# Attention and expert layer: transpose of the combine weights moved within slot 3, expert choice in slot 3, all engine programs without loops

## The reference, cut to what matters

```python
x = x + _L0_attn_ref(_layernorm(x), Wqg, Wkv, Wout)
x = x + _L0_ffn_ref(_layernorm(x), gate_kernel, gate_bias, w_gate, w_up, w_down, ...)
# in the second:
topk_idx, topk_weight = _gate(x, gate_kernel, gate_bias)      # 2 of 4 groups, then 4 of 16 experts
combine = jnp.einsum('nke,nk->ne', onehot, topk_weight)
inter = jax.nn.silu(g) * u                                    # all 16 experts are computed
y = jnp.einsum('ne,enh->nh', combine, jnp.einsum('enm,emh->enh', inter, w_down))
```

## Time and profile before

| | before |
|---|---|
| runs, median (lowest to highest) | 830.85 us (829.86 to 833.11) |
| profiled execution, own time | 831.47 us |
| its span, first to last instruction | 829.5 us |
| PE busy / weight loads | 691.8 us (83%) / 545.1 us (66%) |
| DVE busy | 520.7 us (63%) |
| ACT busy | 434.9 us (52%) |
| POOL busy | 352.7 us (43%) |
| granted clock of PE, mean | 0.920 |
| DMA, mean | 73 GB/s |

### The profile page before, as it was taken

One profiled execution on the slowest core, in us unless ns is written; L12 is line 12 of the kernel. 1 busy time (PEld: TensorE's weight loads), 2 busy tenths in 40 slices (PEclk: granted clock), 3 DMA queues, 4 the chain that ended last, 5 costly groups with the idle time before them and its releaser, 6 DMA issues.

```text
span 829.5 us, 16902 instructions
## 1 busy us (share of the span) xinstructions
PE 691.8 (83%) x5160; PEld 545.1 (66%) x5160; DVE 520.7 (63%) x1739; ACT 434.9 (52%) x986; POOL 352.7 (43%) x368
## 2 busy tenths in 40 slices
PE   1576897979979797988979797997979799797785
PEld 1444476858767685867758585876758587676675
DVE  3545667576666748576575757667475856666654
ACT  2466674565646464564646456464655556453211
POOL 2246563644435353544535264453526444363100
PEclk9878998999989898998989899898989999898898
DMA  8994849091835619092562909174371908300000
GB/s 194 132 144 48 131 87 108 14 144 24 124 48 95 72 60 113 6 139 32 94 72 73 98 18 137 24 113 58 79 87 36 128 1 126 40 15 1 8 7 7
DMA packets 72814, 60.94 MB, mean 73 GB/s; under 512 B 8624, under 2 KB 72496, under 8 KB 72752
## 3 DMA queue, kind: packets, MB, share of 16 engines
q1 hardware_dynamic: 72752, 60.26, 49.4%
HBM read 41.37 MB, written 18.87 MB: 73 GB/s over the span
## 4 chain that ended last, share of the span: by engine, by line
PE 57%; DVE 25%; issue 9%; ACT 4%; DMA 2%; DVEq 1%; POOL 1%; SPq 1%; ACTq 0%; POOLq 0%
PE ps_a L503 11%; PE ps_f L365 8%; PE ps_f L428 7%; PE ps_f L367 6%; PE ps_f L366 6%; PE ps_f L447 5%; PE ps_s L474 5%; PE ps_f L424 4%; DVE norms_m L741 2%; PE ps_f L407 2%; DMA qkt<-qk_rows 2%; DVE it L852 2%; PE ps_f L418 2%; DVE norms_t L661 2%; DVE norms_t L662 2%
## 5 line engine op out<-in xcount | busy, mean ns | idle before, releaser
L334 POOL TENSOR_TENSOR p<-r 128x512 f32<-128x512 f32 x256 | 262.5, 1046 | 392.4 <-ACT r L603 392.4
L603 ACT ACTIVATE r<-ps_s 128x512 f32<-128x512 f32 x256 | 138.5, 596 | 81.0 <-PE ps_s L474 79.8
L503 PE MATMUL ps_a<-p,v 128*64 128x256 f32 x1024 | 143.5, 396 | 3.4 <-DVE big L897 2.2
L897 DVE TENSOR_TENSOR big<-ps_a,wt 128x256 f32<-128x256 f32 x128 | 53.7, 420 | 73.7 <-ACT big L612 51.1
L503 PEld LDWEIGHTS ps_a<-p,v 128*64 128x64 f32 x1024 | 64.4, 138 | 41.7 <-POOL p L334 2.7
L852 DVE TENSOR_TENSOR it<-ps_f,it 128x256 f32<-128x256 f32 x144 | 59.1, 420 | 44.0 <-ACT it L595 41.0
L595 ACT ACTIVATE it<-ps_f 128x256 f32<-128x256 f32 x144 | 55.2, 383 | 50.1 <-PE ps_f L367 47.7
L418 PE MATMUL ps_f<-ident,cs 128*32 128x128 f32 x32 | 9.2, 387 | 83.8 <-DVE cs L787 83.8
L447 PE MATMUL ps_f<-wdown,it 128*128 128x128 f32 x576 | 71.2, 279 | 2.9 <-DVE it L869 1.7
L869 DVE TENSOR_TENSOR it<-ps_f,it 128x512 f32<-128x512 f32 x64 | 44.0, 690 | 44.8 <-PE ps_f L424 44.3
L447 PEld LDWEIGHTS ps_f<-wdown,it 128*128 128x128 f32 x576 | 68.4, 195 | 4.5 <-DVE it L869 1.8
(11 more groups left out here) (153 smaller groups left out, 1607.2 us busy)
## 6 DMA issues: line engine op xcount, KB each, us to landing
qk_rows<-qk_parts SPq DMA_DIRECT2D x16, 1024.0 KB, 4.4
qkt<-qk_rows SPq DMA_DIRECT2D x64, 256.0 KB, 9.5
qkt<-qk_rows SPq DMA_DIRECT2D x128, 128.0 KB, 8.9
x_in<-in_L_attn_tokens SPq DMA_DIRECT2D x16, 128.0 KB, 2.2
x_res<-in_L_attn_tokens SPq DMA_DIRECT2D x16, 128.0 KB, 14.4
out<-o_sb SPq DMA_DIRECT2D x16, 128.0 KB, 14.2
big<-in_L_attn_Wqg SPq DMA_DIRECT2D x1, 640.0 KB, 4.2
big<-in_L_attn_Wkv SPq DMA_DIRECT2D x1, 640.0 KB, 5.3
```

The source lines that it names most:

```text
L334: pool.tensor_tensor(p[h % 4][:], r[h % 2][:], r[h % 2][:], ALU.mult).then_inc(probs_done, 1)
L503: last = pe.matmul(ps_a[k % 2][64 * e:64 * e + 64, 0:N], v[q][:, t, h * DV:(h + 1) * DV], p[h % 4][:, t * N:(t + 1) * N], start=(t == 0), ...
L603: act.activation(r[h % 2][:], ps_s[h % 2][:], ACT.Relu).then_inc(relu_done, 1)
L897: dve.tensor_tensor(aw[ap][:, pair, :], ps_a[pair % 2][:, 0:N], wt[ap][:, pair, :], ALU.mult)\
```

## The change

It takes cT from the head of PE's slot 3 to its end, behind rT, and cB 0 from slot 3 into slot 4, between gu 8 and rB 2. As ACT evacuates in the order of `FILL`, its copy of cT moves too. On DVE `route_experts` moves from slot 2 into slot 3, behind `head_scales`, `gate_up` 5, `gated_heads` of pair 2 and `gate_up` 6; `gate_up` 7 then comes ahead of `value_scales`, and `scale_hidden` 0 goes from the head of slot 4 to a place behind `gate_up` 8. PE, ACT, DVE and POOL are written out for all 20 steps. No instruction is added to or taken from the computation, and no DMA moves.

```diff
-        [("F", "cT", 0), ("F", "gu", 6), ("P", "g", 1), ("F", "gu", 7), ("O", "rT", 0), ("F", "cB", 0)],
-        [("O", "rB", 0), ("O", "rB", 1), ("F", "gu", 8), ("O", "rB", 2), ("O", "rB", 3), ("P", "g", 2)],
+        [("F", "gu", 6), ("P", "g", 1), ("F", "gu", 7), ("O", "rT", 0), ("F", "cT", 0)],
+        [("O", "rB", 0), ("O", "rB", 1), ("F", "gu", 8), ("F", "cB", 0), ("O", "rB", 2), ("O", "rB", 3), ("P", "g", 2)],
...
-        def run_steps(eng, step):
-
-            for s in range(FIRST_STEP, LOOP_FROM):
-                step(s, s % 2, stages(s), s)
-            with eng.Fori(LOOP_FROM // 2, LOOP_TO // 2) as i:
-                step(i * 2, 0, ALL, None)
-                step(i * 2 + 1, 1, ALL, None)
-            for s in range(LOOP_TO, LAST_STEP + 1):
+        def run_flat(step):
+
+            for s in range(FIRST_STEP, LAST_STEP + 1):
                 step(s, s % 2, stages(s), s)
...
@@ DVE
                         if F:
-                            gate_up([4])
-                            route_experts(link_f, fb)
-                            link_f.end()
+                            gate_up([4, 5])
                     if k == 3:
                         if O:
                             head_scales(link_o, b)
                             link_o.end()
+                        gated_heads(k)
                         if F:
-                            gate_up([5])
-                        gated_heads(k)
+                            gate_up([6])
+                            route_experts(link_f, fb)
+                            link_f.end()
+                            gate_up([7])
                         if P_on:
                             value_scales(link_p, s + 1, rq2[pq])
                             link_p.end()
-                        if F:
-                            gate_up([6, 7])
                     if k == 4:
-                        if F:
-                            scale_hidden([0])
                         if O:
                             scale_heads([0, 1])
                         gated_heads(k)
                         if F:
                             gate_up([8])
+                            scale_hidden([0])
                         if O:
                             scale_heads([2, 3])
```

More of the change, by code:

```diff
@@ L351, in step @@
                                 .then_inc(v_normed, 1)
-            run_steps(pool, step)
+            run_flat(step)
         @block.tensor
@@ L506, in step @@
                         last.then_inc(values_done, 1)
-            run_steps(pe, step)
+            run_flat(step)
         @block.scalar
@@ L627, in step @@
                         gates(j, s, q)
-            run_steps(act, step)
+            run_flat(step)
         @block.vector
@@ L1011, in step @@
                                .then_inc(read["x2T"], 1)
-            run_steps(dve, step)
+            run_flat(step)
 _INS = ["L0_attn_tokens", "L0_attn_Wqg", "L0_attn_Wkv", "L0_attn_Wout", "L0_ffn_gate_kernel", "L0_ffn_gate_bias",
```

## The result

The changed kernel takes 826.67 us (median of 17, 819.51 to 830.99), the kernel before 831.15 us (median of 17, 829.86 to 833.80). The ratio is 0.9937 with a 95% interval of 0.9921 to 0.9953. So it is faster by 4.5 us where I had forecast 17, and it just clears the 0.5% that I took as the bound: 826.67 is inside the range of 802 to 827, at its very end. One thing of the runs matters for all that follows. The changed kernel's executions lie 11.5 us apart, those of before 4, and the profiled one, at 819.51 us, is the shortest of the 17.

The account below looks back on a forecast made before the run. PE and DVE taking turns at `cs` was taken as the bound, the loop as second cost. Loop 8, order 5 and last steps 3 us made 16 us off 831.5 (profiled), so 814 us by the median, range 802 to 827.

Parts of the forecast that it names:

- What bounds the kernel: PE and DVE take turns, meeting at PE's wait for `cs`, 83.8 us in 16 waits; loop back edges are second.
- The loop: Writing out the looped steps 4 to 14 was to give 8 us, between 5 and 20.
- DVE's piece: DVE's work ahead of `cs` was to grow by 2.4 us a step, or 1.6 without a second POOL hold.
- PE's piece: From cT to the values of pair 4: 9.35 us before, 5.7 after plus 0.42 per us at half clock.
- The new waits: PE was to wait some 45 us for `cs`, about 14 for `rs` at rT, 15 for `gate_up` 3 at gu 6.
- The clock: Half clock (1.2 GHz) behind cT was to average 2 us a full step, costing 11 us over 13 steps.
- the gain of 16: New order's gain before half clock's cost: 1.25 us in each of 13 full steps, steps 2 to 14.
- the slower rival: Clock drops as cT is released, half clock lasts 6.5 us on dense slots 3 and 4: 839 us, chance 0.08.
- The clock did not stay high by itself: Rival that PE, its idle time in three pieces, keeps the high clock: 27 us gained, 803 us, chance 0.22.
- Only the loop pays: Rival that half clock behind cT or more POOL holds make the new order worth nothing: 823 us, chance 0.18.
- No effect: Rival that loading flat programs stalls each step as a back edge does now: 830 us, chance 0.07.

Follow-up runs that it names:

- flat_only: The kernel before with all programs written out and nothing else changed: 823.16 us, ratio 0.9908 to the kernel before.
- after_again: The changed kernel run once more, unedited, to profile a common execution: median 825.92 us, profiled execution 829.15 us.
- flat_warm29: The kernel before, written out, with 29 spare matmuls in PE's wait for `cs`: 793.67 us, ratio 0.9540 to the kernel before.
- after_warm: The changed kernel with 18 spare matmuls on PE ahead of cT's wait: 798.17 us, ratio 0.9599 to the kernel before.
- pe_only: The changed kernel with `route_experts` put back in slot 2 on DVE, PE's new order kept: 794.23 us, ratio 0.9542 to the kernel before.
- inter: The changed kernel with `route_experts` split, its MAX8 and MATCH_REPLACE8 part beside POOL's squares, the rest behind `head_scales`: 790.43 us, ratio 0.9499 to the kernel before.

## Why the prediction was right or wrong

**What bounds the kernel** held. PE and DVE take turns at `cs`, and each kernel that made `cs` earlier or used the wait gained by it.

**The loop** held, in its size too. I had 8 us; `flat_only` measured 8.2. As forecast, DVE catches up most of each 4.3 us: in the kernel before, a full step with a back edge takes 48.3 to 48.4 us from cT to cT, one without 46.9 to 47.2.

**DVE's piece** held. 2.4 us were forecast and 7.4 against 5.0 us measured, with POOL's hold at L775 and at the cast, 0.6 and 0.8 us of it. I had left open whether cast or copy would be held: it is the cast. The rule of the Trainium skill ("SBUF — State Buffer", Who interferes with whom) names both, and the trace agrees.

**PE's piece** held. I had 5.7 us from cT to the values of pair 4 plus 0.42 us for each us at half clock. In `after_again` it took 287.75 - 282.11 = 5.64 us at full clock, and the longer kinds of step cost 0.40 us for each us at half clock. The new waits came out near the forecast: 42 us for `cs` (forecast some 45), 10 new ones for `rs` (14), 20 at gu 6 (15).

**The clock is the step that failed.** I wrote: "I estimate 2 us of half clock behind cT on average". By the lengths of the twelve full steps above 45.36 us, at 0.40 us each, it was (47.21 - 45.36) / 0.40 = 4.6 us in `after_again` and (46.69 - 45.36) / 0.40 = 3.3 us in the shortest execution. In my own sum 4.6 us instead of 2 take 13 x 0.42 x 2.6 = 14 us from the gain of 16; `after_again` took 829.15 us against my 815.5 for a profiled execution, 14 us more. The estimate leaned on the pause: 5 us of it now bring 2.6 to 5.9 us of half clock, so nearly 3 us, I thought, would bring less. What the runs showed is that a pause of 2.65 us brought as much as one of 5 us, or nothing, with the same waits of PE and the same rows of DVE ahead of it. And because the clock falls late, 1.1 us before cT in step 9, nearly all of the half clock lies on work. That is what the slower rival described. In eight of the twelve full steps of `after_again` it was some 5.7 us, above the 5.2 us from which that rival was to decide (by its own formula that point is 5.0 us); the average stayed below. The whole new order, PE's and DVE's together, is indeed slower by 3 us, and the loop's 8 us hide it.

**A second point was in the numbers, and I did not say it.** My terms for full clock were 5.0 + 7.7 = 12.7 us before and 5.0 + 2.4 + 5.7 = 13.1 us after. The order was 0.4 us a step worse from the start, and `flat_warm29` against `after_warm` measured 0.42. The whole gain that I gave the order was half clock that would go away, 4 us less 2 in each step. By the step lengths it hardly did: `flat_only` has a mean full step of 46.89 us against 44.87 at full clock, an estimate of (46.89 - 44.87) / 0.40 = 5 us of half clock, against 4.6 in `after_again`. The one term that I could not read from a row carried all of the gain. I also took the move of `route_experts` for a part of the exchange and did not work out what PE's order is worth without it; `pe_only` did.

**The rivals.** The clock did not stay high by itself (0.22); held high by spare matmuls it gave 798 us, where that rival had 803. "Only the loop pays", 823 us at 0.18, was the nearest: right in the loop's worth, but the order costs something on top. "No effect" (0.07) had the flat programs stall as they load; DVE shows no such pause, 0.3 us of issue in all.

The Trainium skill ("TensorE: Matmul & The Clock Gate", Why this matters for your kernels) names idle gaps between bursts of matmuls as what drops the clock. The trace agrees that the longer gap drops it more often: with 1.03 us before cT four of twelve full steps had half clock, with 2.65 us eleven did (`after_again`). Both gaps are shorter than those that the page warns of, so here the measurement decides. That the pause was no longer a single one of 5 us did not help.

## What to carry to other kernels

When an edit moves a wait, split the before and after sums into what they are at full clock and what half clock adds; if the gain is all in the second part, it is a bet on the clock, and a few spare matmuls in the wait show within one run what the bet is worth. Moving work out from behind a wait only pays if the chain that ends the wait does not grow by as much: here three PE jobs (2.2 us) came out and four DVE pieces (2.4 us with POOL's hold) went in. When a change moves work on two engines, run each move alone: here PE's was worth 29 us on top of the flat programs, and that of `route_experts` on DVE cost 32. Before lengthening a chain of small VectorE operations, look which of them fall beside a GpSimd instruction, and put there the ones that it does not hold.

## What the runs showed of the hardware

- A pause of TensorE of 2.65 us, with a pause of 0.67 us and two small matmuls (0.38 us) ahead of it, was followed by 5.7, 3.5 or 0 us at 1.2 GHz in steps of the same program. In `inter`, where the last pause is 1.10 us, four of twelve full steps still had some. What decides it in the single step stays open.
- Keeping TensorE busy with matmuls whose result is thrown away made the same program 28 us faster (798.2 against 826.7 us).
- MAX8 and MATCH_REPLACE8 over SBUF are not held by a running GpSimd tensor_tensor (0.18 and 0.17 us beside it in `inter`, as without it), while an operation with two SBUF inputs (0.78 us for 0.18), a cast (0.95 for 0.18) and a tensor_scalar (0.72 for 0.17) are, the first two at 32 elements a partition, the last at 2 (L834 before).
- A hardware loop's back edge cost DVE 4.3 us of issue each, but taking the loop out gave only 8 us in all, since DVE caught up in slots 0 and 1, where it otherwise waits 3.2 us for ACT.
